# Statistics of batches 2 to 6 moved into the state-space layer, normalized rows of queries and router written by GpSimd, queries copied out of PSUM by ScalarE alone

## What is computed

```python
x = x + ssm(_layernorm(x), ...)          # projection, causal conv, SSM over 2 chunks of 128, 64 heads
x = x + xattn(_layernorm(x), ctx, ctx)   # 32 query heads of 16, 8 key heads, softmax over 256 keys
x = x + ffn(_layernorm(x), ...)          # router picks 2 of 8 experts per token, gate/up/down
```

## Time and profile before

| what | value |
|---|---|
| median of 3 runs | 1400.34 us (1399.75 to 1400.81) |
| the profiled execution, its own time | 1394.34 us |
| its span | 1392.4 us |
| TensorE busy | 1286.9 us, 92% |
| VectorE busy | 822.8 us, 59% |
| ScalarE busy | 705.9 us, 51% |
| GpSimd busy | 580.8 us, 42% |

### The profile page before, as it was taken

One profiled execution on the slowest core, in us unless ns is written; L12 is line 12 of the kernel. 1 busy time (PEld: TensorE's weight loads), 2 busy tenths in 40 slices (PEclk: granted clock), 3 DMA queues, 4 the chain that ended last, 5 costly groups with the idle time before them and its releaser, 6 DMA issues.

```text
span 1392.4 us, 23244 instructions
## 1 busy us (share of the span) xinstructions
PE 1286.9 (92%) x7783; PEld 739.6 (53%) x7783; DVE 822.8 (59%) x1840; ACT 705.9 (51%) x1350; POOL 580.8 (42%) x871
## 2 busy tenths in 40 slices
PE   6799999999999999888888888889999999999996
PEld 4567777767676767553334334234444444444443
DVE  5898888787878778578988898661111111111111
ACT  2767676777767666744778767641111111111110
POOL 1465556665656556672333334341222222222221
PEclk9999999999999999987999999989999999999999
DMA  9000000000000000002001010023344344344222
GB/s 351 24 8 5 8 6 9 5 8 5 8 6 8 5 4 9 9 1 102 13 28 44 32 32 33 32 77 106 77 137 136 58 133 143 80 103 136 46 46 31
DMA packets 40354, 73.41 MB, mean 53 GB/s; under 512 B 18544, under 2 KB 22896, under 8 KB 39216
## 3 DMA queue, kind: packets, MB, share of 16 engines
q1 hardware_dynamic: 30304, 48.49, 10.0%
q0 software_dynamic: 8736, 20.61, 7.9%
q10 hardware_dynamic: 1200, 2.82, 0.5%
HBM read 149.30 MB, written 19.99 MB: 122 GB/s over the span
## 4 chain that ended last, share of the span: by engine, by line
PE 66%; DVE 18%; issue 6%; ACT 5%; POOL 3%; DMA 1%; SPq 1%; POOLq 0%; DVEq 0%; ACTq 0%
PE work_ps L572 12%; PE gate_ps L1573 10%; PE up_ps L1573 10%; PE down_ps L1557 9%; PE work_ps L644 7%; PE work_ps L577 4%; DVE maxes L1263 3%; DVE conv L771 3%; PE work_ps L1089 3%; PE mturn_ps L577 2%; DVE decay L767 2%; PE work_ps L664 2%; PE work_ps L1080 2%; ACT prob L1161 1%; PE work_ps L652 1%
## 5 line engine op out<-in xcount | busy, mean ns | idle before, releaser
L572 PE MATMUL work_ps<-xnT,w_in 128*128 128x256 f32 (+1 forms) x1216 | 289.1, 386 | 4.3 <-DVE xdt L902 2.4
L572 PEld LDWEIGHTS work_ps<-xnT,w_in 128*128 128x128 f32 (+1 forms) x1216 | 226.8, 193 | 54.8 <-issue 21.9
L767 POOL TENSOR_TENSOR decay<-decay,cbm 128x512 f32<-128x512 f32 x128 | 183.8, 1437 | 147.4 <-ACT decay L762 144.3
L1661 POOL DMA_INDIRECT out_dram<-y_out,ids x39 | 61.9, 1587 | 334.3 <-DVE row_w L1625 228.7
L1263 DVE TENSOR_REDUCE maxes<-work_ps 128x2 f32<-128x512 f32 x256 | 166.0, 681 | 28.7 <-PE work_ps L1065 27.7
L1161 ACT ACTIVATE prob<-work_ps 128x512 f32<-128x512 f32 x256 | 142.3, 609 | 66.2 <-PE work_ps L1080 65.6
L1640 DVE TENSOR_TENSOR act<-gelu,up_ps 128x512 f32<-128x512 f32 x39 | 26.8, 688 | 251.8 <-PE up_ps L1573 251.8
L762 ACT ACTIVATE decay<-decay 128x512 f32<-128x512 f32 x256 | 162.1, 640 | 12.5 <-DVE xnT L1212 5.4
L758 ACT ACTIVATE decay<-work_ps 128x512 f32<-128x512 f32 x256 | 138.7, 600 | 38.4 <-PE work_ps L652 37.8
L1573 PE MATMUL gate_ps<-w_e,xgT 128*128 x312 | 140.5, 593 | 1.4 <-ACT xgT L1590 1.0
L1557 PE MATMUL down_ps<-w_e,actT 128*128 x312 | 140.4, 593 | 0.8 <-ACT actT L1603 0.8
(11 more groups left out here) (271 smaller groups left out, 1947.7 us busy)
## 6 DMA issues: line engine op xcount, KB each, us to landing
w_e<-c_experts_dram SPq DMA_DIRECT2D x39, 3072.0 KB
normed_tokens<-r_xn SPq DMA_DIRECT2D x17, 256.0 KB, 2.2
out_dram<-x_sb SPq DMA_DIRECT2D x17, 256.0 KB, 2.5
x_sb<-x_dram SPq DMA_DIRECT2D x1, 3072.0 KB, 17.4
w_in<-c_w_inT_dram ACTq DMA_DIRECT2D x1, 2560.0 KB, 11.8
w_in<-c_w_inT_dram SPq DMA_DIRECT2D x1, 2048.0 KB, 9.7
w_out<-c_w_outT_dram SPq DMA_DIRECT2D x1, 2048.0 KB, 22.5
RT<-cum_scratch SPq DMA_DIRECT2D x32, 48.0 KB
```

The lines of the kernel that those rows point to most:

```text
L572: m = e.matmul(ps[0:width, at:at + L], w_in[:, k, col:col + width], xnT[b % 2][:, k, :], start=(k == 0), stop=(k == KD - 1))
L767: return e.tensor_tensor(four(decay[s % NDECAY]), four(decay[s % NDECAY]), cb, ALU.mult)
```

## The change

- `q_bn`, `q_stats`, `q_newton` of batches 2 to 6 are put into the mixer, each batch by itself, behind the `x_add` of its two tiles. Batch 7's stay in attention, alone (two tiles), in the slots 2 to 5 of batch 5; batches 0 and 1 stay as they were. `a_bn` grows from 4 to 16 tiles.
- `q` and `r_xn` (all but the last batch's `r_xn`) go from ScalarE to GpSimd, as one operation with two scalars per partition (`normed_row`).
- The half of the queries that VectorE copied (`q_copy_v`) goes to ScalarE.

```diff
@@ attention_slots
-        if b and b % 2 == 0:
-            for t in range(2 * TPB):
-                put(r + t, ("q_bn", b * TPB + t))
-            put(r + 4, ("q_stats", b // 2))
-            put(r + 5, *[("q_newton", b // 2, i) for i in range(3)])
+        if b == NB - 1:
+            for t in range(TPB):
+                put(r + 2 + t, ("q_bn", b * TPB + t))
+            put(r + 4, ("q_stats", b))
+            put(r + 5, *[("q_newton", b, i) for i in range(3)])
...
-            put(r + 17 + 5 * t, ("q_copy_v", b, t, 0), ("q_turn", b, t, 1))
-            put(r + 19 + 5 * t, ("q_copy_s", b, t, 1))
+            put(r + 17 + 5 * t, ("q_copy", b, t, 0), ("q_turn", b, t, 1))
+            put(r + 19 + 5 * t, ("q_copy", b, t, 1))
@@ whole_order
+    for b in range(2, NB - 1):
+        end = PER_B * (b + 1) + 16
+        slots += [(end - NG + NG * t, 1, [("q_bn", b * TPB + t)]) for t in range(TPB)]
+        slots += [(end + 2, 1, [("q_stats", b)])] + [(end + 3 + 2 * i, 1, [("q_newton", b, i)]) for i in range(3)]
@@ scalar_attention
-            elif stage == "q":
-                b, t = key
-                tile = b * TPB + t
-                e.wait_ge(*done("q_newton", b // 2, 2))
...
-                e.activation(a_xn[t][:, :], x_sb[:, tile, :], ACT.Identity, bias=a_rows[:, 3, tile:tile + 1], scale=a_rows[:, 1, tile:tile + 1]).then_inc(piece_done[stage], 1)
...
-            elif stage == "q_copy_s":
+            elif stage == "q_copy":
...
-                e.activation(qT[b % 3][:, NPR // 2:NPR, t * P:(t + 1) * P], work16("q_turn", b, t, half).rearrange("p (k j) -> p k j", j=P), ACT.Copy).then_inc(piece_done[stage], 1)
+                e.activation(qT[b % 3][:, half * NPR // 2:(half + 1) * NPR // 2, t * P:(t + 1) * P], work16("q_turn", b, t, half).rearrange("p (k j) -> p k j", j=P), ACT.Copy).then_inc(piece_done[stage], 1)
@@ vector_attention
-                if tile >= 2 * TPB and tile % (2 * TPB) == 0:
-                    e.wait_ge(*done("q_stats", tile // (2 * TPB) - 1))
-                e.bn_stats(a_bn[:, tile % (2 * TPB), :], x_sb[:, tile, :]).then_inc(piece_done[stage], 1)
+                e.wait_ge(*done("x_add", tile))
+                e.bn_stats(a_bn[:, tile, :], x_sb[:, tile, :]).then_inc(piece_done[stage], 1)
@@ gpsimd_attention
+        def normed_row(e, o, tile, rows):
+            return e.tensor_scalar(o[:, :], x_sb[:, tile, :], rows[:, 1, tile:tile + 1], rows[:, 3, tile:tile + 1], ALU.mult, ALU.add)
...
+            elif stage == "q":
+                b, t = key
+                e.wait_ge(*done("q_newton", b if b >= 2 else 0, 2))
+                if b:
+                    e.wait_ge(*done("q_lo", b - 1, t))
+                else:
+                    e.wait_ge(*done("xn_turn", NB - 1, 1))
+                normed_row(e, a_xn[t], b * TPB + t, a_rows).then_inc(piece_done[stage], 1)
+            elif stage == "r_xn":
+                b, t = key
+                if b < NB - 1:
+                    e.wait_ge(*done("r_newton", b))
+                    if b:
+                        e.wait_ge(*done("r_turn", b - 1, t))
+                        e.wait_ge(store_tokens[t], 16 * b)
+                    normed_row(e, r_xn[t], b * TPB + t, r_rows).then_inc(piece_done[stage], 1)
```

More of the change, by code:

```diff
@@ L205, in bank_use @@
     if stage == "q_turn":
-        return (stage, *key), ("q_copy_s" if key[2] else "q_copy_v", *key)
+        return (stage, *key), ("q_copy", *key)
     if stage == "product":
@@ L394, in layer_kernel @@
         a_xn = [sb(top, "a_xn0", [P, DIM]), xn]
-        a_bn = sb(top, "a_bn", [P, 2 * TPB, 6])
+        a_bn = sb(top, "a_bn", [P, NT, 6])
         a_mv = sb(top, "a_mv", [P, NT, 2])
@@ L1061, in tensor_attention @@
                     e.wait_ge(*done("k_copy", b, 1))
-                    e.wait_ge(*done("q_copy_v", b, 1, 0))
-                    e.wait_ge(*done("q_copy_s", b, 1, 1))
+                    e.wait_ge(*done("q_copy", b, 1, 0))
+                    e.wait_ge(*done("q_copy", b, 1, 1))
                 for hh in range(2):
@@ L1170, in scalar_attention @@
                 b, t = key
[L1171 to L1174, removed]
+                if b == NB - 1:
+                    e.wait_ge(*done("last_newton"))
+                    e.wait_ge(*done("r_turn", b - 1, 1))
                     e.wait_ge(store_tokens[t], 16 * b)
-                if b == NB - 1:
                     e.wait_ge(*done("last_center", t))
                     e.activation(r_xn[t][:, :], a_xn[t][:, :], ACT.Copy, scale=last_rows[:, 1, 0, t:t + 1]).then_inc(piece_done[stage], 1)
-                    return
-                e.activation(r_xn[t][:, :], x_sb[:, tile, :], ACT.Identity, bias=r_rows[:, 3, tile:tile + 1], scale=r_rows[:, 1, tile:tile + 1]).then_inc(piece_done[stage], 1)
             elif stage == "last_center":
@@ L1236, in vector_attention @@
                 tile, = key
-                if tile >= 2 * TPB and tile % (2 * TPB) == 0:
-                    e.wait_ge(*done("q_stats", tile // (2 * TPB) - 1))
-                e.bn_stats(a_bn[:, tile % (2 * TPB), :], x_sb[:, tile, :]).then_inc(piece_done[stage], 1)
+                e.wait_ge(*done("x_add", tile))
+                e.bn_stats(a_bn[:, tile, :], x_sb[:, tile, :]).then_inc(piece_done[stage], 1)
             elif stage == "q_stats":
-                j, = key
-                ts = slice(2 * TPB * j, 2 * TPB * (j + 1))
+                ts = queried(*key)
                 e.wait_ge(*done("q_bn", ts.stop - 1))
-                for t in range(2 * TPB):
-                    m = e.bn_aggr(a_mv[:, ts.start + t, :], a_bn[:, t, :])
+                for t in range(ts.start, ts.stop):
+                    m = e.bn_aggr(a_mv[:, t, :], a_bn[:, t, :])
                 own.settle(m)
@@ L1253, in vector_attention @@
                 e.tensor_copy(kT[b % 3][:, :, t * P:(t + 1) * P], work16("k_turn", b, t).rearrange("p (k j) -> p k j", j=P)).then_inc(piece_done[stage], 1)
[L1254 to L1257, removed]
             elif stage == "max_fold":
@@ L1402, in vector_attention, with queried @@
                 e.tensor_tensor(own_tile[c][:, :, :], tiles, wide(tile_of[:, c, :]), ALU.is_equal).then_inc(piece_done[stage], 1)
+        def queried(j):
+            return slice(TPB * j, TPB * (j + 1)) if j else slice(0, 2 * TPB)
+        def normed_row(e, o, tile, rows):
+            return e.tensor_scalar(o[:, :], x_sb[:, tile, :], rows[:, 1, tile:tile + 1], rows[:, 3, tile:tile + 1], ALU.mult, ALU.add)
         def placed_in(t):
@@ L1428, in gpsimd_attention @@
                 j, step = key
-                ts = slice(2 * TPB * j, 2 * TPB * (j + 1))
+                ts = queried(j)
                 e.wait_ge(*(done("q_newton", j, step - 1) if step else done("q_stats", j)))
```

## The result

The changed kernel takes **1444.95 us** (median of 4 runs, 1440.71 to 1445.49) against 1400.33 before (1399.75 to 1400.81): ratio 1.0326, 95% interval 1.0299 to 1.0353, 44.6 us slower. The forecast was 12.4 slower, 1412.7 with a range to 1432. The sign was right; the size was not. The mean granted clock of TensorE fell from 0.977 to 0.950.

What follows compares the result with a forecast made beforehand. Attention was taken as bound by queues waiting for each other, the mixer by TensorE. Terms -3.4 + 4.2 + 9.1 - 4.8 + 4.8 + 1.0 + 1.5 = +12.4 us on 1400.34 gave 1412.7 us, range 1396 to 1432.

Steps and rivals of the forecast that it cites:

- A of batches 1 to 3: Attention from `r_turn` (router's first transpose) to the next `attend`: bound by TensorE, near 21.3 us against 22.13 without statistics.
- experts: The experts stage: untouched, 0.
- TensorE's clock: Behind gaps of about 3.7 us in B, 3.5 us at 1.2 GHz lose at least 1.2; four new ones: +4.8.
- Batch 4: Attention, batch 4: A +3.8 for batch 7's 14 statistics steps on GpSimd, B +5.3 with `place` queued; together +9.1.
- Stretch B: Attention from `attend` to `r_turn`: GpSimd's longer chain makes it 13.4 us against 10.66, 2.7 longer.
- Relief of VectorE and ScalarE: Attention: VectorE loses a copy per tile, ScalarE trades two rows for two copies; -0.8 for six batches: -4.8.
- Batches 5 and 6: Attention, batches 5 and 6: no term of their own; -0.8 of relief for batch 5, 0 for batch 6.
- Mixer and its end: Mixer: products meeting late ones, +1.0 (0 to 4); its end: ScalarE's copies and `q_hi` waiting for GpSimd, +1.5 (0 to 4).
- Statistics: Start of attention: the first set of statistics (batches 2 and 3) is gone, -3.4.
- VectorE as the bound: Rival in attention: VectorE bounds it and the change is faster, 1384.6 us; chance 0.15.
- Cancelling: Rival in attention: B grows by 2.7, A falls to 20.07, the clock holds, 1400.3 us; chance 0.14.
- The dear row: Rival on GpSimd: a normalized row takes 2.7 us in place of 0.69, +30, 1442.7 us; chance 0.14.

Runs made afterwards that it cites:

- the filled gaps: The change with 18 matmuls of 128x128x512 that compute nothing put before the router's first transpose of each batch: 1423.44 us, ratio 1.0156.
- the fastest version: The kernel with the statistics alone, batch 7's statistics put two stretches earlier and its three steps apart: 1392.9 us, ratio 0.9954.
- the statistics alone: The change with both normalized rows back on ScalarE and query copies split again between VectorE and ScalarE: 1396.55 us, ratio 0.9965.
- the reordered kernel: The change with query rows put ahead of `attend` and the router's rows right behind the root (both reorderings): 1404.55 us, ratio 1.0011.
- the router's rows first: The change with the router's two normalized rows ahead of tile 1's queries in the order, nothing else: 1448.07 us, ratio 1.0334.
- statistics and copies: The change with both normalized rows back on ScalarE, all query copies staying on ScalarE: 1399.97 us, ratio 0.9972.

## Why the prediction was wrong in size

The steps of the sum beside the two profiled executions, in us. "Forecast" is the share of the 12.4; relief and clock are put to the stretches they were meant for.

```
stretch                          before    after   change   forecast
to batch 0's first max           592.12   597.97     +5.9       +2.5
to the first attend               91.54    89.16     -2.4       -3.4
B of batches 0 to 3               40.50    56.54    +16.0      +13.1
A of batches 1 to 3               75.34    76.70     +1.4       -7.7
A ahead of batch 4's attend       29.56    34.98     +5.4       +4.2
B of batch 4                      11.27    16.78     +5.5       +5.3
A behind it                       22.24    29.32     +7.1       -0.8
batch 5's B, A                    33.18    37.20     +4.0       -0.8
batch 6's B, A                    24.82    32.05     +7.2        0
experts                          471.8    472.1      +0.3        0
```

- **TensorE's clock** is the step that failed: "3.5 us at 1.2 GHz in a stretch that is 91% TensorE lose at least 1.2. Four new ones: +4.8." That the clock falls behind the new gaps was right: it did behind all four of 4.07. Three of the four behaved as priced, with 3.3 us of low clock and some 1.5 us lost. The first did not: 16.5 us low, and an A of 29.41 in place of 22.12. And three long ones came where nothing was charged, behind batch 4 (16.4 us low), 5 (13.6) and 6 (14.3), by the same working from the rows above. These four cost some 22 us more than the sum has, an estimate from their A: 7.3 - 1.2 in the first, and 7.1, 4.0 and 5.0 against the rows of before. The run with the filled gaps puts the clock's whole share at 24 us or more in place of 4.8; that is some 19 of the 32 us between forecast and result. "(Batch 4 has one already)" misread its row: that low clock lay almost wholly in B, the A behind it had 0.99, and 0.72 with the change. The price had no upper end in the range either, though the trace of before holds a longer example than both of the earlier trace rows, with no wait of TensorE over 1.75 us in the 8 us ahead of it:

```profile
646.20:656.30 10.10, 9.05 (x40) 2.05 (x40) 9.73 (x22) 5.52 (x13) 4.60 (x18) 0.50 0.56 168
```

- **Stretch B**: right in its chain, +13.1 against +16.0. A row is 0.77, not 0.69, but most of the 0.7 is the 0.51 in front of the 14 steps: the sum let them start 5.65 behind `attend`, while VectorE's part was ready for them only at 5.86 before the change and at 6.22 with it. The Trainium skill's "roughly line-rate" (GPSIMD Engine Reference, section 4.1), an estimated 0.43, is further off here.
- **Relief of VectorE and ScalarE** (-4.8): not there. At full clock the A is 22.12 with the copies split and ScalarE's rows, and 22.12 with ScalarE's copies, GpSimd's rows and filled gaps. TensorE's 2 us of waiting in A don't go with VectorE's load, which is 18.1 us in the one and 17.2 in the other.
- **Batch 4**: +10.9 for A and B, +9.5 forecast with relief and clock. Right as a sum; the 5.90 us for which TensorE stands still within B were not foreseen, but GpSimd's chain is the longer one there (16.78 against 16.6 forecast).
- **Batches 5 and 6** were priced at relief or nothing; the working stopped at batch 4. Batch 6's router rows queue behind `place` on GpSimd (B 14.18 against 11.99; 11.98 in the run with the router's rows on ScalarE), and the low clock follows. Batch 5 got no longer a wait than before (1.98 us against 2.31); its A is 27.29 here, and 27.36 in the fastest version, which has no row on GpSimd. So its +4.0 is not shown to be the change's doing.
- **Mixer and its end**: +5.9 for 2.5. The eight runs with batch 0's query rows on GpSimd have the first `max` at 596.56 to 597.97, the two that have these rows and all their copies on ScalarE at 595.32 and 595.71, the three with the statistics alone between 593.72 and 596.96. So the three parts overlap and can't be told apart; together they cost 4.4 to 5.9 us against the one profile of before. The rows of batch 0 have no term in the sum.
- **Statistics**: the set that left the start of attention gave 2.4, of 3.4, in this one execution.
- **Rivals.** VectorE as the bound: no, in no run. Cancelling: no; yet the reordered kernel, at 1.0011, shows that the rows on GpSimd need not cost more than some 5 us. The dear row: its time (1442.7) is the nearest of all to the result, its cause is wrong (0.77 us, not 2.7). A rival "the gaps cost a long low clock each" would have come near the result with the right cause, 12.4 + 4 x 6 = some 36 us slower (6 being 28.24 - 22.12, above), and none was written.

## What to carry to other kernels

Before work moves to an idle engine, list that engine's queue: query rows of 0.8 us each cost 28 us in all (the run with them alone), because one of every two stood behind 3.8 us of tiny steps and in front of what TensorE and ScalarE needed, and with both kinds of rows a few slots earlier they cost some 5 us. When a producer moves across engines, look for every wait that hangs on it, on all consumers, since the second shows only when the first is gone. Price a new gap on TensorE with an upper end from the longest low-clock stretch in the trace, not by the mildest alone, and charge it to every batch whose wait moves; half the damage here was done after the waiting was over.

## What the hardware showed that I had not expected

Gaps of one length, followed by the same instructions, had three outcomes: no fall (22.12 us for the A, gaps of 2.05 and 2.56), 1.2 GHz for about 3.5 us (23.6, gap 4.07), or for 13 to 17 us (28 to 29.4, gaps of 2.05, 2.56 and 4.07), with TensorE busy throughout the two low parts shown behind the gaps of the change. Two waits close together, of 1.00 and 1.58 us, were followed by the long kind too (A of 31.5 in the run with the router's rows first). Where a wait of 1.0 us or less was the only one at the start of an A of batches 1 to 3, only short falls came in it, and those began some 6 us into it: twice with the statistics alone, once with statistics and copies, twice with both reorderings. One kind of stretch A, the same 182 matmuls, thus varies by 6 us in one execution (28.24 against 22.12), and what decides it is not the gap's length alone. The section "Why this matters for your kernels" of the Trainium skill's TensorE: Matmul & The Clock Gate page warns of pauses; that agrees with the fall behind every gap of 4.07 us, and no run here shows what chooses between the short and the long stretch. It stays open.
